# A transformer layer with relative attention and routed experts: other parts of the skewed tables, split terms stored once, shares spread by PE

## The chip, the core and the metric

The kernel runs on one core of a Trainium2 chip. The core has TensorE (PE, matrix products), VectorE (DVE), ScalarE (ACT), GpSimd (POOL), and SyncE (SP), which here issues nearly all DMAs; 16 DMA engines move the data between DRAM and on-chip memory (SBUF), and a DMA adds 16 to a semaphore when it has landed. The metric is the device time of one execution in microseconds; the figure of a kernel is the median of its runs.

## The reference

The input x is 4 batches x 1024 tokens x 256 channels. With LN a layer norm without scale:

```python
def attention(h):                        # h = LN(x)
    q, k, v = (heads(h @ W + b) for W, b in ((Wq, bq), (Wk, bk), (Wv, bv)))   # 16 heads of 16
    pos_k = heads(rel_embeddings @ Wk + bk)                                  # 128 buckets
    c2p[i, j] = (q @ pos_k.T)[i, bucket(i - j) + 64]     # clipped to 0..127, one bucket for all far keys
    p2c[i, j] = (k @ pos_k.T)[j, bucket(i - j) + 64]
    ctx = softmax((q @ k.T + c2p + p2c) / sqrt(48)) @ v
    out = ctx @ Wo + bo + h
    return LN(out) * ln_scale + ln_bias
def ffn(h):                              # every token goes to its best of 8 experts
    e = argmax(h @ Wr + br)
    return sum over i of relu((h if i == e else 0) @ W1[i] + b1[i]) @ W2[i] + b2[i]
x = x + LN(attention(LN(x)))
x = x + LN(ffn(LN(x)))
```

## The kernel before, in words

The program runs five stages, one after the other; each has a block of instructions for every engine, with the order of work written out by hand and semaphores between the engines.

**spread** makes the gathered position rows for all heads (pick_d). **project** takes 8 groups of 512 tokens: x is normalised (xn), turned, and multiplied by Wq, Wk and Wv. q and k are wanted to nearly full float32 precision in bfloat16 products, so each is split into three bfloat16 parts (hi, mid, lo). A product needs six terms, so that q is stored six times in split_d in the order hi hi hi mid mid lo, and k in the order that goes with it (QSLOTS and KSLOTS): 12 stores a group from L363. far_d (4 stores, L369) holds the products with the two buckets for far keys, v_d (L374) the values. POOL adds bo to xn, and SP stores that sum in xn_d (L352) for the residual later. On DVE, L435 and L403 make the rests for mid and lo, L400 and L406 those of the far rows. On SP every group's stores stand in one queue: xn_d of group s + 2, split_d and far_d of group s - 1, v_d of group s.

**attend** works on 64 units; a unit is one head of one batch. It is cut into 8 query tiles of 128. For each tile PE makes a table of 128 rows x 256 positions for each of q and k (L712, L714), and ACT copies it out of PSUM (L859). The table must be shifted by one column more in each row, which is done in DRAM: SP writes it to skew_d with one pitch (skew_write, L655) and reads it back with a pitch smaller by one (skew_read, L665, whose wait is at L662). A unit's table is written in two parts, tiles 0 to 3 and 4 to 7, and read in two parts, tiles 0 to 2 and 3 to 7 (PIECES), each for two tables. POOL then sets the edges of the bands (L926 to L942, five operations a part) and copies side values (L914). PE makes the scores (L733) and adds the bands by transposes (L740), DVE takes maxima (L814) and levels the bands (L833), PE transposes (L756, L763), ACT exponentiates (L865), PE multiplies with the values (L777). The row maxima of a unit are split in three bfloat16 parts by POOL (split_top, L952 to L962) and turned by PE (turn_top, L785), which stands in PE's order among the tables of a later unit.

SP's order for each unit u is: read part 1 of unit u + 1; write part 0 of unit u + 2; load the split and far rows of unit u + 4 (load_unit: two loads of 96 rows at L637, three of few rows at L642, into one of six buffers); store the result of unit u - 2 (L671); read part 0 of unit u + 2; write part 1 of unit u + 2. All of these pass through one queue, in which an instruction that waits holds all behind it.

**mix** takes 16 groups of two tiles: the sums of the probabilities are inverted, stored in share_d, and loaded back spread over the channels (share), beside heads, the stored xn and x. DVE multiplies heads by share (share_heads, L1156), PE multiplies by Wo (project_out, L1331), DVE adds the stored xn (residual, L1149), three norms and the routing follow. SP loads b1 (L1116) and, in its first eight steps, W2 (L1119). PE's constant_rows (L1361) gathers the constant part of the experts at steps 12 and 16. **experts** gathers the tokens by expert and computes the second layer.

## Time and profile before

| | |
|---|---|
| median of 3 runs | 2007.51 us (2007.21 to 2009.05) |
| profiled execution | 2003.63 us, span in the trace 2001.7 us, mean granted clock 0.916 |
| busy | PE 85%, PEld 58%, DVE 68%, ACT 56%, POOL 53% |
| DMA | 453.36 MB, mean 226 GB/s |
| stages | spread to 38, project to 200, attend to 1492, mix to 1688, experts to 2001 us |

The span is the trace's stretch from first to last work; the time of the execution is a little longer. Busy shares are means over stages that have different limits. In the page's own view of 40 slices the change between stages can be seen:

```profile
PE   1882389999999999999999999999973674999997
...
PEclk6996589999999999999999999999996675999998
```

One digit is one fortieth of the span, about 50 us, and 9 is 90% or more. Attention is the long row of nines in the middle, and mixing the dip after it.

### The profile page before, as it was taken

The page shows a single profiled execution, that of the slowest core. Times are in us where ns is not written, and L with a number is a line of the kernel's source. Part 1 is how long each engine was busy: PE and PEld are TensorE (multiplying, and loading weights), DVE is VectorE, ACT ScalarE, POOL GpSimd, SP SyncE. Part 2 cuts the span into 40 slices and gives each one's busy share as a digit, 9 for nine tenths or more (in the row PEclk, how much of TensorE's full clock was granted, in tenths as well). Part 3 has the DMA queues.
Part 4 walks back from the last instruction along what each step waited for, and adds up shares of the span by engine and source line. Part 5 has one row for each costly group of instructions (what it writes and reads, how often), then busy time and mean ns, then how long its engine had stood idle before and what let it go on. Part 6 is the DMA issues. An engine that isn't in the chain of part 4 may idle for free. (4 is left out here: it accounts for less than half of the span.)

```text
span 2001.7 us, 40568 instructions
## 1 busy us (share of the span) xinstructions
PE 1698.0 (85%) x13688; PEld 1159.6 (58%) x13688; DVE 1370.7 (68%) x3938; ACT 1121.8 (56%) x2233; POOL 1069.1 (53%) x1268
## 2 busy tenths in 40 slices
PE   1882389999999999999999999999973674999997
PEld 1451156565656566566565666566532464999996
DVE  1673188788888788898798899899843553343343
ACT  1672257676767677677677777677751460222221
POOL 0210267676777667667576777777711451233332
PEclk6996589999999999999999999999996675999998
DMA  4598778777777777777877777787718852676772
GB/s 113 188 303 274 225 250 262 246 237 251 245 261 248 256 247 240 257 254 245 265 237 251 249 261 250 240 272 246 235 44 215 284 176 86 198 212 215 223 219 78
DMA packets 320826, 453.36 MB, mean 226 GB/s; under 512 B 35132, under 2 KB 260303, under 8 KB 320526
## 3 DMA queue, kind: packets, MB, share of 16 engines
q1 hardware_dynamic: 308034, 415.25, 65.2%
q10 hardware_dynamic: 7596, 21.10, 3.4%
q0 software_dynamic: 4992, 14.43, 1.9%
q8 instruction: 112, 1.84, 0.4%
q14 instruction: 92, 0.75, 0.1%
HBM read 257.32 MB, written 193.65 MB: 225 GB/s over the span
## 5 line engine op out<-in xcount | busy, mean ns | idle before, releaser
L865 ACT ACTIVATE t_probsT<-t_flip 128x512 f32<-128x512 f32 x1024 | 619.2, 607 | 242.7 <-PE t_flip L756 117.5
L814 DVE TENSOR_REDUCE t_most<-t_scores 128x1 f32<-128x640 f32 (+1 forms) x512 | 436.7, 853 | 169.8 <-PE t_scores L740 166.5
L833 DVE TENSOR_SCALAR t_band<-t_band,t_top 128x384 f32<-128x384 f32 (+1 forms) x512 | 383.8, 750 | 0.0
L859 ACT COPY t_table<-t_table_ps 128x512 f32<-128x512 f32 x512 | 298.2, 582 | 70.7 <-issue 41.1
L777 PE MATMUL t_sum_ps<-t_probsT,t_vals 128*32 128x256 f32 x4096 | 329.5, 394 | 0.2 <-ACT t_probsT L865 0.2
L926 POOL TENSOR_TENSOR t_near<-t_near,t_masks 128x384 f32<-128x384 f32 (+1 forms) x128 | 146.8, 1147 | 338.9 <-DMA t_near<-skew_d 336.4
L942 POOL TENSOR_TENSOR t_near<-t_near,t_masks 128x768 f32<-128x768 f32 (+1 forms) x128 | 272.4, 2129 | 0.0
L763 PE MATMUL t_flip<-t_masks,t_band 128*128 128x128 f32 x1408 | 263.0, 276 | 0.0
L818 DVE CUSTOM_DVE_ANT_0 t_band<-t_scores,t_near 128x384 f32<-128x384 f32 (+1 forms) x512 | 262.1, 512 | 0.0
L740 PE MATMUL t_scores<-t_masks,t_near 128*128 128x128 f32 x1408 | 243.5, 277 | 7.1 <-POOLq L945 7.1
L733 PE MATMUL t_scores<-t_after,t_quest 105*128 105x256 bf16 (+3 forms) x1024 | 244.9, 289 | 2.6 <-DVE t_most L818 2.4
L740 PEld LDWEIGHTS t_scores<-t_masks,t_near 128*128 128x128 f32 x1408 | 182.7, 143 | 46.6 <-POOLq L945 8.7
L712 PE MATMUL t_table_ps<-t_rows,t_quest 96*128 96x256 bf16 x512 | 143.5, 280 | 69.1 <-DMA t_before<-far_d 49.8
L733 PE MATMUL t_scores<-t_before,t_quest 105*128 105x256 bf16 (+3 forms) x768 | 195.0, 294 | 0.0
L763 PEld LDWEIGHTS t_flip<-t_masks,t_band 128*128 128x128 f32 x1408 | 164.7, 143 | 4.8
L756 PE MATMUL t_flip<-t_quest,t_before 108*128 108x512 bf16 (+3 forms) x512 | 161.4, 316 | 0.8 <-ACT t_probsT L865 0.7
L756 PE MATMUL t_flip<-t_quest,t_after 108*128 108x512 bf16 (+3 forms) x512 | 158.7, 310 | 1.2 <-DMA t_quest<-t_topT 0.8
L1606 PE MATMUL e_hid_ps<-e_xT,e_w 128*128 128x128 f32 x1248 | 148.0, 278 | 5.6 <-DMA e_total<-total_d 5.2
L1606 PEld LDWEIGHTS e_hid_ps<-e_xT,e_w 128*128 128x128 f32 x1248 | 147.5, 194 | 8.2 <-issue 5.5
L939 POOL TENSOR_TENSOR t_near<-t_near,t_masks 128x384 f32<-128x384 f32 (+1 forms) x128 | 145.5, 1137 | 0.0
L714 PE MATMUL t_table_ps<-t_rows,t_after 96*128 96x256 bf16 x512 | 142.9, 279 | 0.0
L1588 PE MATMUL e_out_ps<-w_all,e_hid 128*128 x624 | 141.0, 379 | 0.0
(186 smaller groups left out, 2343.7 us busy)
## 6 DMA issues: line engine op xcount, KB each, us to landing
skew_d<-t_table SPq DMA_DIRECT2D x128, 1024.0 KB, 8.9
t_near<-skew_d SPq DMA_DIRECT2D x128, 640.0 KB, 6.2
t_near<-skew_d SPq DMA_DIRECT2D x128, 384.0 KB, 4.8
e_w<-in_L_ffn_W_dram ACTq DMA_DIRECT2D x39, 512.0 KB
e_w<-in_L_ffn_W_dram SPq DMA_DIRECT2D x39, 512.0 KB
split_d<-p_part SPq DMA_DIRECT2D x32, 384.0 KB
t_after<-split_d SPq DMA_DIRECT2D x64, 192.0 KB
t_quest<-split_d SPq DMA_DIRECT2D x64, 192.0 KB
```

The lines of the kernel that those rows point to most:

```text
L733: nc.tensor.matmul(out[:, at:at + size], quest[i][0:XROWS, t * P:(t + 1) * P], keys[0:XROWS, piece[0] * P:piece[0] * P + size], start=at % ...
L740: last = nc.tensor.matmul(out[:, (j - lo) * P:(j - lo + 1) * P], near[n % 2][:, 1, j, (t - j + 1) * P:(t - j + 2) * P], ident, start=False ...
L756: last = nc.tensor.matmul(out[:, (a - lo) * P:(z - lo) * P], keys[:, j * P:(j + 1) * P], quest[i][:, a * P:z * P], start=first, stop=False ...
L763: last = nc.tensor.matmul(out[:, (t - lo) * P:(t - lo + 1) * P], band[n % 2][:, t, at:at + P], ident, start=False, stop=True, is_transpose ...
L777: last = nc.tensor.matmul(sum_ps[32 * g:32 * g + 32, 0:2 * P], vals[b % 2][:, j, h * VDIM:h * VDIM + 32], probsT[s % 3][:, g * 2 * P:(g + ...
L814: nc.vector.tensor_reduce(most[:, c, 1:2], out[:, wide:S], AX.X, ALU.max)
L818: nc.vector.tensor_tensor_reduce(band[n % 2][:, t, 0:wide], out[:, 0:wide], near[n % 2][:, 0, t, at:at + wide], 1.0, -3.0e38, ALU.add, ALU ...
L833: nc.vector.tensor_scalar(band[n % 2][:, t, 0:wide], band[n % 2][:, t, 0:wide], top[n % 2][:, t:t + 1], None, ALU.subtract).then_inc(level ...
L859: nc.scalar.copy(table[n % 2][:, h, :, u % 4, :], table_ps[:, :, :]).then_inc(table_kept, 1)
L865: nc.scalar.activation(probsT[s % 3][:, half * 512:(half + 1) * 512], flip_ps[half][:, :], ACT.Exp, scale=SCALE).then_inc(expd, 1)
L942: nc.gpsimd.tensor_tensor(tail, tail, masks[:, 1, :].unsqueeze(1).unsqueeze(1).to_broadcast([P, 2, many, P]), ALU.mult).then_inc(edge_made, 1)
L1606: last = nc.tensor.matmul(hid_ps[s % 2][:, c, :], w1[s % WB][:, f, c * P:(c + 1) * P], xT[s % 2][:, f, :], start=(f == 0), stop=(f == 1))
```

## The change

In **attend** the table of a unit is written in parts of five and three tiles (TILES), and read in parts of four and four (PIECES). POOL's steps for the edges move later, and the split of the maxima, which stood between two parts of the edges, now comes before the second one's first step. The split rows are loaded by six DMAs of 32 rows each instead of two of 96. In **project** each of the three parts is stored once: q's as mid, lo, hi and k's as hi, mid, lo, so that a load finds any pair of neighbours; the pair of one part twice is a step of 0 in the load. far_d gets one store with padding. The sum xn + bo is no longer made or stored, and POOL has nothing to do there. In **mix** the shares are loaded once, as 16 rows, and PE spreads them over the channels by a product with a 0/1 matrix (which), for each group; PE also adds bo, by a product of one row; the residual is made from x and the kept inverse deviations (inv_all, which project now writes for all tokens). W2's loads stand at every second step, and the second constant_rows at step 18. The padding, masks and experts are as they were.

```diff
-QSLOTS = ((0, 1, 3), (3, 1, 2), (5, 1, 1))
-KSLOTS = ((1, 2, 3), (2, 2, 2), (0, 1, 1))
+QSLOTS = ((0, 1, 5), (2, 3), (4,))
+KSLOTS = ((0, 2, 4), (1, 3), (5,))
...
-        split_d = dram("split_d", [2, TERMS, N * DH, S], BF16)
-        far_d = dram("far_d", [2, N, 2, PARTS, S], BF16)
+        split_d = dram("split_d", [2, PARTS, N * DH, S], BF16)
+        far_d = dram("far_d", [B, 4, 32, PARTS, S], BF16)
...                                                       project, SP
-                    sp.wait_ge(xnb_made, g + 1)
-                    sp.dma_start(view(xn_d, g * G * D, [[D, P], [P * D, GT], [1, D]]), xnb[g % 2][:, :, :]
-                                 ).then_inc(xn_out[g % 2], 16)
...
-                        for n, (first, step, many) in enumerate((QSLOTS, KSLOTS)[m // 2]):
-                            at = ((m // 2 * TERMS + first) * (N * DH) + b * D + m % 2 * P) * S + half * G
-                            sp.dma_start(view(split_d, at, [[S, P], [step * N * DH * S, many], [1, G]]),
-                                         part[g % 2][:, n, m, :].unsqueeze(1).to_broadcast([P, many, G])
-                                         ).then_inc(split_out[g % 2], 16)
+                        mine = at + m // 2 * (PARTS * part_at) + m % 2 * (P * S)
+                        takes = ((0, 2, 1), (2, 3, 0)) if m < 2 else ((0, 3, 0),)
+                        for a, z, slot in takes:
+                            sp.dma_start(view(split_d, mine + slot * part_at, [[S, P], [part_at, z - a], [1, G]]),
+                                         part[g % 2][:, a:z, m, :]).then_inc(split_out[g % 2], 16)
...
-                    for m in range(4):
-                        at = (m // 2 * N + b * H + m % 2 * 8) * 2 * PARTS * S + half * G
-                        sp.dma_start(view(far_d, at, [[PARTS * S, 16], [S, PARTS], [1, G]]),
-                                     far_part[g % 2][32 * m:32 * m + 16, :, :]).then_inc(far_out[g % 2], 16)
+                    sp.dma_start(view(far_d, b * (P * PARTS * S) + half * G, [[PARTS * S, P], [S, PARTS], [1, G]]),
+                                 far_part[g % 2][:, :, :]).then_inc(far_out[g % 2], 16)
...                                                       project, POOL
-                nc.gpsimd.tensor_tensor(xnb[g % 2][:, :, :], xn[g % NB][:, :, :],
-                                        bo_b[:, :].unsqueeze(1).to_broadcast([P, GT, D]), ALU.add).then_inc(xnb_made, 1)
...                                                       attend
-    PIECES = ((0, 3), (3, QT))
-    EDGES = ((0, 3), (3, QT - 1))
+    TILES = ((0, 5), (5, QT))
+    PIECES = ((0, 4), (4, QT))
+    EDGES = ((0, 4), (4, QT - 1))
...
+            pair, one, both = [[S, 2 * DH], [1, S]], [[S, DH], [1, S]], [[part, 2], [S, DH], [1, S]]
...
-                for dst, side_at in ((after[i], TERMS * part), (quest[i], 0)):
-                    sp.dma_start(dst[0:KROWS, :], view(split_d, side_at + n * (DH * S), [[part, TERMS], [S, DH], [1, S]])
-                                 ).then_inc(hats_in[i], 16)
...
+                for dst, src_at, dims in ((after[i][0:2 * DH, :], at_k, both), (after[i][2 * DH:4 * DH, :], at_k, both),
+                                          (after[i][4 * DH:KROWS, :], at_k, [[2 * part, 2]] + one),
+                                          (quest[i][0:2 * DH, :], at_q + part, [[0, 2]] + one),
+                                          (quest[i][2 * DH:4 * DH, :], at_q + 2 * part, [[0, 2]] + one),
+                                          (quest[i][4 * DH:KROWS, :], at_q, both)):
+                    sp.dma_start(dst, view(split_d, src_at, dims)).then_inc(hats_in[i], 16)
...
-                sp.wait_ge(table_kept, n * QT + 4 * h + 4)
+                lo, hi = TILES[h]
+                sp.wait_ge(table_kept, n * QT + hi)
...
-                    sp.wait_ge(scored, (n - 2) * QT + 4 * h + 4)
-                    sp.wait_ge(seen, (n - 2) * QT + 4 * h + 4)
+                    sp.wait_ge(scored, (n - 2) * QT + TILES[h][1])
+                    sp.wait_ge(seen, (n - 2) * QT + TILES[h][1])
...
-            steps = ((2, 0, (0, 1)), (3, 0, (2,)), (4, 0, (3,)), (5, 0, (4,)),
-                     (6, 1, (0, 1)), (7, 1, (2,)), (8, 1, (3,)), (9, 1, (4,)))
+            steps = ((3, 0, (0, 1)), (4, 0, (2,)), (5, 0, (3,)), (6, 0, (4,)), (8, 1, (0, 1)), (9, 1, (2, 3)), (10, 1, (4,)))
...                                                       mix
-                for k in range(2):
-                    n = g // 4 * H + k * 8
-                    sp.dma_start(share[i][:, k, :], view(share_d, n * S + g % 4 * (2 * P), [[S, 8], [0, DH], [1, 2 * P]])
-                                 ).then_inc(heads_in[i], 16)
...
-                sp.dma_start(xn[i][:, :, :], rows_of(xn_d, g)).then_inc(xn_in[i], 16)
...
+            sp.dma_start(share[:, :, :], view(share_d, 0, [[S, H], [H * S, B], [1, S]])).then_inc(share_in, 16)
...
-                nc.vector.tensor_tensor(y1[g % BUFS][:, :, :], out_ps[g % 2][:, :, :], xn[g % BUFS][:, :, :],
-                                        ALU.add).then_inc(y1_made, 1)
+                for t in range(G):
+                    tile = g * G + t
+                    last = nc.vector.scalar_tensor_tensor(y1[g % BUFS][:, t, :], xt[g % XBUFS][:, t, :],
+                                                          inv_all[:, tile:tile + 1], out_ps[g % 2][:, t, :], ALU.mult, ALU.add)
...
+                    last = nc.tensor.matmul(out_ps[g % 2][:, t, :], masks[0:1, 3, :], bo_row[:, :], start=False, stop=True)
...
+                for k in range(2):
+                    last = nc.tensor.matmul(share_ps[g % 2][:, k, :], which[:, k, :], share[:, b, at:at + G * P],
+                                            start=True, stop=True)
```

On SP in the even part of attention, one unit of before (skew_d is the table in DRAM, t_near the shifted band, t_after and t_quest the rows of keys and queries):

```order
L665 DMA t_near<-skew_d 128x5x256 x2
L655 DMA skew_d<-t_table 256x1x1024
L637 DMA t_after<-split_d 96x1x1024
L637 DMA t_quest<-split_d 96x1x1024
L642 DMA t_quest<-far_d 6x1024
L642 DMA t_after<-far_d 3x1024
L642 DMA t_before<-far_d 3x1024
L671 DMA ctx_d<-t_made 128x256
L665 DMA t_near<-skew_d 128x3x256 x2
L655 DMA skew_d<-t_table 256x1x1024
```

And the same place after the change:

```order
L658 DMA t_near<-skew_d 128x4x256 x2
L648 DMA skew_d<-t_table 256x1x1280
L628 DMA t_after<-split_d 32x1x1024 x3
L628 DMA t_quest<-split_d 32x1x1024 x3
L634 DMA t_quest<-far_d 6x1024
L634 DMA t_after<-far_d 3x1024
L634 DMA t_before<-far_d 3x1024
L664 DMA ctx_d<-t_made 128x256
L658 DMA t_near<-skew_d 128x4x256 x2
L648 DMA skew_d<-t_table 256x1x768
```

The order of kinds is the same; two loads became six, and the parts of the reads and writes have other sizes.

On POOL in attention, from the first part's third edge step on, before:

```order
L934 TENSOR_TENSOR t_near<-t_near,t_side 128x4x128
L952 CAST t_top_part<-t_top 128x8
L954 TENSOR_TENSOR t_top_rest<-t_top,t_top_part 128x8
L957 CAST t_top_part<-t_top_rest 128x8
L959 TENSOR_TENSOR t_top_rest<-t_top_rest,t_top_part 128x8
L962 CAST t_top_part<-t_top_rest 128x8
L914 COPY t_side<-t_table 128x2x4
L939 TENSOR_TENSOR t_near<-t_near,t_masks 128x4x128
L942 TENSOR_TENSOR t_near<-t_near,t_masks 128x2x4x128
```

And after:

```order
L936 TENSOR_TENSOR t_near<-t_near,t_masks 128x2x4x128
L946 CAST t_top_part<-t_top 128x8
L948 TENSOR_TENSOR t_top_rest<-t_top,t_top_part 128x8
L951 CAST t_top_part<-t_top_rest 128x8
L953 TENSOR_TENSOR t_top_rest<-t_top_rest,t_top_part 128x8
L956 CAST t_top_part<-t_top_rest 128x8
L908 COPY t_side<-t_table 128x2x3
L920 TENSOR_TENSOR t_near<-t_near,t_masks 128x3x128
L923 TENSOR_TENSOR t_near<-t_near,t_side 128x3x128
L928 TENSOR_TENSOR t_near<-t_near,t_side 128x3x128
```

The split of the maxima (t_top_part, t_top_rest) stood inside the second part's edge steps (sizes of four tiles), behind its L926, and stands now between the first part's last step and the second part's first one (L920, three tiles).

On SP in the projection stage, one group of before:

```order
L363 DMA split_d<-p_part 128x3x512
L363 DMA split_d<-p_part 128x2x512
L363 DMA split_d<-p_part 128x512
L363 DMA split_d<-p_part 128x3x512
L363 DMA split_d<-p_part 128x2x512
L363 DMA split_d<-p_part 128x512
...
L369 DMA far_d<-p_far_part 48x1x512 x4
L374 DMA v_d<-p_v_1 128x4x288
```

And of after:

```order
L361 DMA split_d<-p_part 128x2x512
L361 DMA split_d<-p_part 128x512
L361 DMA split_d<-p_part 128x2x512
L361 DMA split_d<-p_part 128x512
L361 DMA split_d<-p_part 128x3x512 x2
L364 DMA far_d<-p_far_part 384x1x512
L369 DMA v_d<-p_v_1 128x4x288
```

A group had 12 stores of split_d and 4 of far_d and has now 6 and 1; the store of xn_d between the groups is gone.

## Rows read from the trace of the kernel before

**Rows 1.** Stretch: busy PE, PEld, DVE, ACT, POOL; clock; DMA share; GB/s. Then L763.

```profile
300.00:1440.00 1140.00, 1087.80 (x9996) 684.91 (x9992) 990.45 (x2839) 829.45 (x1595) 813.06 (x1008) 0.99 0.77 250
L763 PE MATMUL t_flip<-t_masks,t_band 128*128 128x128 f32 x1301 | 243.4, 276 | 0.0
```

**Rows 2.** Waits of SP's queue, 300 to 1440 us: sum, count, longest.

```profile
SPq L662 <- DMA skew_d<-t_table: 695.8, 115, 8.3
```

**Rows 3.** Timeline of SP, 795 to 830 us: start, duration.

```profile
797.43 0.93 SPq L665 DMA_DIRECT2D t_near<-skew_d  x2
798.46 0.56 SPq L655 DMA_DIRECT2D skew_d<-t_table  x1
799.07 0.77 SPq L637 DMA_DIRECT2D t_after<-split_d  x1
...
808.00 0.91 SPq L665 DMA_DIRECT2D t_near<-skew_d  x2
809.02 0.57 SPq L655 DMA_DIRECT2D skew_d<-t_table  x1
816.39 0.93 SPq L665 DMA_DIRECT2D t_near<-skew_d  x2
```

**Rows 4.** Waits of PE and POOL, 300 to 1440 us.

```profile
PE t_table_ps L785 <- POOL t_top_part L962: 45.1, 44, 4.4
POOL t_near L926 <- DMA t_near<-skew_d: 307.5, 106, 6.1
```

**Rows 5.** Busy time in short stretches, columns as in rows 1.

```profile
808.00:808.25 0.25, 0.00 (x0) 0.00 (x0) 0.25 (x2) 0.00 (x0) 0.17 (x2) 1.00 0.38 147
...
808.50:808.75 0.25, 0.00 (x0) 0.00 (x0) 0.24 (x1) 0.00 (x0) 0.17 (x2) 1.00 0.39 139
...
810.00:811.00 1.00, 1.00 (x7) 0.85 (x6) 0.00 (x0) 0.47 (x1) 1.00 (x2) 0.50 0.82 213
813.00:814.00 1.00, 1.00 (x13) 0.42 (x6) 0.96 (x6) 0.13 (x1) 0.26 (x1) 0.80 1.02 415
```

**Rows 6.** Timeline of PE at 215 us.

```profile
214.98 0.37 PE L712 MATMUL t_table_ps<-t_rows,t_quest 96*128 96x256 bf16 x1 [49.79 <-DMA t_before<-far_d]
```

**Rows 7.** Timeline of SP, 155 to 200 us.

```profile
156.85 9.76 SPq L363 DMA_DIRECT2D split_d<-p_part  x12
...
169.30 0.58 SPq L374 DMA_DIRECT2D v_d<-p_v  x1
...
192.82 2.60 SPq L369 DMA_DIRECT2D far_d<-p_far_part  x4
199.86 0.35 SPq L676 DMA_DIRECT2D t_rows<-pick_d  x1
```

**Rows 8.** Timelines of PE and DVE in the projection stage.

```profile
69.76 3.70 PE L524 MATMUL p_qk_ps<-p_xT,p_wq 128*128 128x512 f32 x8
...
82.15 1.13 PE L524 MATMUL p_qk_ps<-p_xT,p_wq 128*128 128x512 f32 x2
70.12 2.28 DVE L435 TENSOR_TENSOR p_rest<-p_qk,p_part 128x2048 f32<-128x2048 f32 x1
...
79.93 2.86 DVE L406 TENSOR_TENSOR p_far_part<-p_far_rest,p_far_part 128x512 bf16<-128x512 f32 x1
...
85.77 2.28 DVE L435 TENSOR_TENSOR p_rest<-p_qk,p_part 128x2048 f32<-128x2048 f32 x1
170.79 2.29 DVE L435 TENSOR_TENSOR p_rest<-p_qk,p_part 128x2048 f32<-128x2048 f32 x1 [4.36 <-ACT p_part L501]
...
177.25 0.69 DVE L406 TENSOR_TENSOR p_far_part<-p_far_rest,p_far_part 128x512 bf16<-128x512 f32 x1
```

**Rows 9.** Mixing stage: a wait, busy time, PE by line (x, busy, mean ns).

```profile
DVE m_headsT L1156 <- DMA m_share<-share_d: 51.2, 14, 12.8
1500.00:1690.00 190.00, 109.63 (x520) 86.89 (x520) 90.26 (x330) 65.75 (x148) 60.86 (x50) 0.63 0.61 180
L1331 PE MATMUL m_out_ps<-m_wo,m_headsT 128*128 128x256 f32 x128 | 49.8, 556 | 63.3 <-DVE m_headsT L1156 63.3
```

More of the change, by code:

```diff
@@ L83, in constants @@
     steps[:, ET + 8 + P:] = np.arange(NT)[None, :] * P + np.arange(P)[:, None] + 1
+    heads = np.zeros((H, 2, P), np.float32)
+    for h in range(H):
+        heads[h, h // 8, h % 8 * DH:h % 8 * DH + DH] = 1.0
     sel = np.zeros((P, E), np.float32)
@@ L208, in _ @@
             for tab in range(2):
-                for n, (first, step, many) in enumerate((KSLOTS, QSLOTS)[tab]):
-                    for slot in range(first, first + step * many, step):
+                for n, slots in enumerate((KSLOTS, QSLOTS)[tab]):
+                    for slot in slots:
                         for c in range(2):
@@ L265, in _, with project @@
             nc.vector.tensor_tensor(part[:, 2, :, :, :], rest[:, :, :, :], part[:, 1, :, :, :], ALU.subtract).then_inc(dve_made, 1)
-def project(nc, sem, spent, x, Wq, bq, Wk, bk, Wv, bv, bo, c_masks, posT_d, xn_d, split_d, far_d, v_d):
+def project(nc, sem, spent, x, Wq, bq, Wk, bk, Wv, bv, c_masks, posT_d, split_d, far_d, v_d, inv_all):
     G = 512
@@ L347, in _ @@
                 load(g)
[L348 to L355 removed]
+            for s in range(NG + 1):
+                if live(s + XB):
+                    load(s + XB)
                 g = s - 1
@@ L559, in attend @@
     BUFS = 6
-    HATS = 5
+    HATS = 9
     FAR = KROWS + PARTS
@@ L586, in attend @@
         vals = [sb(f"vals{i}", [P, QT, VROW]) for i in range(2)]
-        table = [sb(f"table{i}", [P, 2, 2, 4, SPOT]) for i in range(2)]
+        table = [sb(f"table{i}", [P, 2, QT, SPOT]) for i in range(2)]
         side = [sb(f"side{i}", [P, 2, QT]) for i in range(2)]
@@ L1016, in mix @@
         out_ps = [ps(f"out_ps{i}", [P, G, D]) for i in range(2)]
+        share_ps = [ps(f"share_ps{i}", [P, 2, G * P]) for i in range(2)]
         xf_ps = ps("xf_ps", [P, 2, G * P])
@@ L1107, in _ @@
                      (wr[:, :, :], Wr.rearrange("(k p) n -> p k n", p=P)),
-                     (br_b[:, :], row(br, E)), (steps[:, :], c_steps)]
-            assert len(loads) == 7
+                     (br_b[:, :], row(br, E)), (steps[:, :], c_steps),
+                     (which[:, :, :], c_heads), (bo_row[:, :], view(bo.tensor, 0, [[D, 1], [1, D]]))]
+            assert len(loads) == 9
             for dst, src in loads:
                 sp.dma_start(dst, src, allow_slow_non_contiguous=True).then_inc(loaded, 16)
-            for g in range(BUFS):
-                load(g)
+            load(0)
+            load(1)
+            sp.wait_ge(inverse_made, 1)
+            sp.dma_start(share_d[:, :].rearrange("n (a v) -> (n a) v", a=2), inverse[:, :]).then_inc(share_out, 16)
+            load(2)
+            sp.wait_ge(share_out, 16)
+            sp.dma_start(share[:, :, :], view(share_d, 0, [[S, H], [H * S, B], [1, S]])).then_inc(share_in, 16)
+            load(3)
             for dst, src in [(b1_sb[:, :, :], b1.rearrange("e (c p) -> p e c", p=P)), (b2_sb[:, :], b2),
```

155 lines of the change are left out of this document (76 added, 79 removed).

## The prediction

> **What bounds the kernel now.** I read the granted-clock and busy table by stretch first. From 300 to 1440 us, where the attention stage runs evenly, PE is busy 1087.8 of 1140.0 us at clock 0.99 and the DMA engines 0.77 [rows 1]. That looks like a PE-bound stage, so I read the waits of the SP queue for the same stretch: its reads back of the skewed tables (L662) waited 695.8 us for the writes (skew_d<-t_table) to land, 115 times [rows 2]. The SP timeline shows why this decides [rows 3]: read 797.43, write 798.46, unit loads from 799.07, read 808.00, write 809.02, the next read 816.39. Every write follows its read in about 0.1 us and every read waits for the write ahead of it. This is a closed ring of DMAs with nothing of PE in it: 816.39 - 797.43 = 18.96 us for one unit (a unit is one head of one batch, 64 in all). The stretch holds 1301 / 22 = 59.1 units by the transposes of L763, 22 to a unit [rows 1], so a unit takes 19.3 us and PE's own work is 1087.8 / 59.1 = 18.4 us of it. PE follows the ring: its one large stall is 45.1 us at L785, for the split of the row maxima on POOL, which itself sits behind POOL's wait for t_near from DMA, 307.5 us [rows 4].
>
> The next view is the same table in quarters of a microsecond just after a large write has landed. At 808.00 only unit loads are left to run, for the read issued at 808.00 shows from 809 on; there the share of the 16 DMA engines is 0.38, at 147 GB/s, then 0.39 at 139 at 808.5 [rows 5]. 6 / 16 = 0.375. At 813 us, with table traffic, the share is 1.02 at 415 GB/s. The load's source pattern is `[[part, 6], [S, 16], [1, S]]`: its outermost size is 6, and six engines carry it, at 147 / 6 = 24.5 GB/s each.
>
> **The change, part by part.**
> Unit loads, the largest term. The two loads of 96 rows become six of 32 rows, each with an outermost size of 2 in the source (the middle of the change). The bytes stay: 2 x 96 x 2048 = 393,216. If the outermost size sets the engines, as 6 gave six, each of these runs on two; and I take the same two for all six, since the two loads of before share one set of six (two sets would show 0.75). Then it is 393,216 / (2 x 24.5 GB/s) = 8.0 us, in place of 393,216 / 147 GB/s = 2.7 us. In the ring they stand between the large write and the next read, and on the engines that carry them the read's packets stand behind them, so the difference, 5.3 us, comes onto the ring. Its cover is nothing: the ring has no slack [rows 3]. From below: the two slow engines do their part of the read while the other fourteen are idle, and could do it faster; the 64 rows of it per engine take 4 us at the mean rate, so at most 1 us comes back, 4.3. From above: 393,216 bytes at 2 x 23 GB/s (139 / 6, the lowest share of such a window that I take) is 8.5 - 2.7 = 5.8. I take 5.3, because the other side of the packet queue is equally loaded before and after. 62 of the 64 rounds of the ring have a load: 62 x 5.3 = +329 us (267 to 360). The first unit's load delays the first table too, for which PE waits until 214.98 [rows 6]: +5.
>
> The Trainium skill has this as a rule (DMA: Bandwidth & Descriptors, "Why a DMA increments its semaphore by 16 and not by 1"): a DMA runs on the largest number of engines up to 16 that divides the outermost size of both patterns. For 6 and 96 that is six, which the share of 0.38 bears out; for 2 and 32 it is two, always the lowest-numbered, which no run here has shown yet. By it the term is the same.
>
> The parts of five and three tiles move bytes and no sum: before, a read of 5 + write of 4, then a read of 3 + write of 4; now 4 + 5 and 4 + 3. Nine tiles and seven tiles either way: 0. Four more issues a unit on SP, at 0.77 us each [rows 3], run inside the 9.5 us wait for the large write: 0, at most +1 us a round if they outlast it.
>
> Maxima ahead of masking: POOL's split no longer stands behind the part that waits longest for t_near. The 45.1 us of stall at L785 [rows 4] go, and what is late next is the same DMA at the scores (L740): the ring sets the round, so 0 in the even stretch. Once, at the end, PE is some tiles further ahead: -4 us (0 to -8). The first write needs a fifth tile: +1.
>
> Projection stage. SP issues without a gap from 156.85 to the end: 12 stores of split_d 9.76 us, 4 of far_d 2.60, one of v_d 0.58, 13 us a group, the last at 192.82 + 2.60, and attention begins at 199.86 [rows 7]. The last lo part is ready at 177.25, when L406 follows it on DVE [rows 8], so SP is 18 us late. Now a group has 6 stores at 9.76 / 12 = 0.81 each, one of far_d and one of v_d, about 6 us: SP is no longer the limit. PE is: a group of it runs from 69.76 to 82.15, 12.4 us. DVE has the same room, since its L406 took 2.86 us beside the POOL addition, which goes, and 0.69 us without it [rows 8]. L435 of group 0 starts at 70.12 and that of group 1 at 85.77, or at 83.6 without the 2.2 us of L406; then 6 x 12.4 to that of group 7 at 158.0, and 6.5 us from there to the end of lo (170.79 to 177.25 in the trace) give 164.5; six stores 4.9, far_d 0.65 and the same 4.4 us to the first DMA of attention: 174.5 against 199.86, -25 us. Bounds: -30 (SP's whole excess and the backlog) and -18 (a group at 13.4 us, as 85.77 less 70.12 without L406's 2.2).
>
> Mixing stage. The loads of m_share and m_xn go. DVE waited 51.2 us for m_share, of which 12.8 behind the load of single b1 words, which stays, and about 10 for the first shares, which a spread by PE behind the same store and load doesn't shorten; 28 us is the most to win. Against it stand 128 more PE passes of 256 columns (the share's and bo's): at the 556 ns of L1331 71 us, on a PE that is busy 109.6 of 190 us at clock 0.63 [rows 9]. At the half clock PE would be the limit, at +5; nearer its full one the steps take 6 to 6.5 us where they took 7.2 over eleven groups. I take -15 (-28 to +5), the middle. W2's loads at every second step and the constant rows at step 18 lie beside this: 0.
>
> **The sum.** The profiled execution took 2003.63 us with 2001.7 of span; 2003.6 - 25 + 5 + 1 + 329 - 4 - 15 = 2294.6. The median of the runs before is 2007.51, 3.9 above it: 2298, say 2300.
>
> **Rivals.**
> Two engines (chance 0.82): the above. Its own range, from the bounds of its terms taken two thirds of the way, is 2235 to 2340.
> The engines don't follow the outermost size, and the loads stay at six or more (0.09). For it: only one size, six, is seen [rows 5]. Against: 0.375 fits no other count. Then 2003.6 - 25 + 2 - 4 - 15 = 1962, +3.9 = 1966, faster. It decides from the point where six small loads take less than 3 us together. Were they to run on all 16, the ring would fall under PE's 18.4 us and PE would set it: 62 x 0.9 less, about 1910.
> The loads run on two engines but on different pairs, or largely beside the tables (0.05): 1 to 3 us a round, 2 x 62 = 124: 2090. For it: queues can interleave; against it: the loads come after the write, not with it [rows 5].
> The clock (0.04): the large stall ended at 809, and at 810 to 811 us PE was granted 0.50, its lower level of 1.2 GHz [rows 5]. With a stall of 6 us in each round the clock could stay at its half. PE's 18.4 us would become 36.8 with the clock always low, over the ring's 24.5; with it low half of the time 27.6, so 2300 + 62 x 3.1 = 2490.
>
> **How the numbers follow.** Two engines, pairs and clock are slower: 0.91, less 0.01 that a half-right mixture lands within 0.2%, which is about what a measurement of this kernel can tell from no change (4 us). Faster 0.09. The range holds 8 in 10: 2210 to 2370 holds nearly all of the first case's 0.82 and leaves out the rest.
>
> **What the profile after would show.** Right: the wait from the small write to its read up from 7.4 to about 12.7 us and from the large write to its read still about 9.5, a round of 24 us, PE busy about 0.75 of the even stretch with its idle time at L740 behind POOL, none at L785; just after the large write a share of 0.12 to 0.13 at 46 to 49 GB/s for several microseconds; attention's first DMA at 175 us; DVE's L406 at 0.7 us; no wait for m_share, and steps of 6 us in mixing. Wrong: a round of 19 us or less, or a share of 0.38 in that window. If the stores of split_d still hold ACT, the 25 us fail alone; if PE's half clock holds in mixing, the 15 do.

## The result and the profile after

| | before | after |
|---|---|---|
| median on the same chip | 2007.36 us | 2223.32 us |
| ratio | | 1.108 (95% interval 1.106 to 1.111) |
| span of the profiled execution | 2001.7 us | 2222.9 us |

The kernel became slower by 11%, where 15% were forecast. By SP's first DMA of each stage the two spans divide as follows; the forecast is the sum of the prediction's terms for that stage.

| stage | before | after | difference | forecast |
|---|---|---|---|---|
| spread and project | 199.9 | 172.3 | -27.6 | -25 |
| attend | 1292.9 | 1498.1 | +205.2 | +331 |
| mix | 196.3 | 239.5 | +43.2 | -15 |
| experts | 312.6 | 313.0 | +0.4 | 0 |

Attention was forecast 126 us too high and mixing 58 us too low. So the total stands inside the range because two errors had opposite signs: with mixing as forecast it would have been 2165, below the range of 2210 to 2370. That part is luck. The rows of after, in the order of the rows of before. The even part of attention first (columns as in [rows 1]):

```profile
300.00:1600.00 1300.00, 1120.12 (x9750) 688.58 (x9749) 969.59 (x2768) 812.98 (x1558) 789.37 (x985) 0.94 0.68 215
```

PE is busy 1120 of 1300 us, 0.86, where it was 0.95, and the DMA engines' share fell from 0.77 to 0.68. The waits of SP's queue there:

```profile
SPq L655 <- DMA skew_d<-t_table: 511.9, 97, 8.8
SPq L648 <- ACT t_table L852: 62.0, 81, 2.4
```

The read still waits above all for the table to land; its waits are 5.3 us each, fewer and shorter than the 6.0 of [rows 2], because SP itself now issues for longer. SP's timeline of one unit (start, duration):

```profile
1008.20 0.91 SPq L658 DMA_DIRECT2D t_near<-skew_d  x2
1009.21 0.55 SPq L648 DMA_DIRECT2D skew_d<-t_table  x1
1009.82 1.94 SPq L628 DMA_DIRECT2D t_after<-split_d  x3
1011.80 3.71 SPq L628 DMA_DIRECT2D t_quest<-split_d  x3
...
1017.35 0.35 SPq L664 DMA_DIRECT2D ctx_d<-t_made  x1
1019.27 1.15 SPq L658 DMA_DIRECT2D t_near<-skew_d  x2
1020.52 1.86 SPq L648 DMA_DIRECT2D skew_d<-t_table  x1
1030.77 0.91 SPq L658 DMA_DIRECT2D t_near<-skew_d  x2
```

The wait from the large write (1009.21, five tiles) to its read (1019.27) is 10.1 us, that from the small write (1020.52) to its read (1030.77) 10.3; [rows 3] had 9.5 and 7.4. Over 300 to 1400 us the means are 9.0 and 10.3, where before had 9.7 and 7.4: the cost of the slow loads appears behind the small write, where it was forecast, as 10.3 and not 12.7. A unit takes 22.6 us. The six loads take 5.65 us to issue where two took 1.6. The ring also has PE in it now: SP waits 62.0 us in 1300, about 1 us a round, for ACT's copy of the table (L648 above), and before that wait was 4 us in 1100. The shares in this unit, columns as in [rows 5]:

```profile
1008.00:1009.00 1.00, 1.00 (x10) 0.75 (x7) 0.97 (x4) 0.80 (x2) 1.00 (x2) 1.00 0.00 0
1019.00:1020.00 1.00, 1.00 (x11) 0.83 (x9) 1.00 (x1) 0.71 (x2) 1.00 (x1) 1.00 0.14 51
1027.00:1028.00 1.00, 1.00 (x15) 0.64 (x8) 1.00 (x2) 0.74 (x3) 0.00 (x0) 1.00 0.14 48
1028.00:1029.00 1.00, 1.00 (x9) 0.65 (x7) 0.65 (x5) 1.00 (x3) 0.25 (x1) 1.00 0.14 55
1029.00:1030.00 1.00, 1.00 (x14) 0.55 (x14) 0.87 (x2) 0.50 (x1) 1.00 (x2) 1.00 0.12 46
1030.00:1030.50 0.50, 0.50 (x6) 0.35 (x4) 0.47 (x3) 0.30 (x1) 0.50 (x2) 1.00 0.02 6
```

From 1027 to 1030 the share is 0.12 to 0.14 at 46 to 55 GB/s: two of 16 engines carry all that is left, and the read follows when they end. The forecast had this share just after the large write; it is there at 1019 and lasts for several microseconds only behind the small one. The 0.14 at 1019 us is a second thing to see: two engines work on while the large write's landing is answered and the next read starts up, a pause in which nothing else runs. At 1008 us the same pause has a share of 0.00. PE and POOL wait as follows:

```profile
POOL t_near L920 <- DMA t_near<-skew_d: 482.3, 63, 11.8
PE t_scores L733 <- POOLq L939: 172.6, 58, 5.8
```

L785 (now L778) is gone from PE's list, as forecast, and the scores wait for POOL's edges, behind DMA, in its place. The projection stage, SP and one row of DVE:

```profile
154.58 2.98 SPq L361 DMA_DIRECT2D split_d<-p_part  x6
157.60 0.86 SPq L364 DMA_DIRECT2D far_d<-p_far_part  x1
158.51 1.07 SPq L369 DMA_DIRECT2D v_d<-p_v  x1
162.77 2.97 SPq L361 DMA_DIRECT2D split_d<-p_part  x6
...
172.29 0.34 SPq L669 DMA_DIRECT2D t_rows<-pick_d  x1
```

```profile
80.13 0.69 DVE L400 TENSOR_TENSOR p_far_part<-p_far_rest,p_far_part 128x512 bf16<-128x512 f32 x1
```

A group's stores take 2.98 + 0.86 + 1.07 = 4.9 us on SP, against 12.9 in [rows 7], and attention begins at 172.29. The additions on far rows are at 0.69 us at once. The mixing stage, two stretches and PE's lines:

```profile
1750.00:1770.00 20.00, 20.00 (x50) 13.04 (x50) 8.61 (x34) 8.10 (x20) 9.14 (x8) 0.50 0.53 162
1790.00:1810.00 20.00, 20.00 (x56) 13.95 (x56) 8.61 (x34) 7.42 (x17) 6.49 (x6) 0.50 0.51 158
```

```profile
L1326 PE MATMUL m_out_ps<-m_wo,m_headsT 128*128 128x256 f32 x128 | 63.8, 651 | 4.2 <-DVE m_headsT L1151 4.2
L1328 PE MATMUL m_out_ps<-m_bo_row,m_masks 1*128 1x256 f32 x64 | 37.9, 692 | 0.0
L1336 PE MATMUL m_share_ps<-m_share,m_which 16*128 16x256 f32 x64 | 29.6, 615 | 24.3 <-DMA m_share<-share_d 24.3
```

PE is busy for the whole of each stretch at clock 0.50, its lower level, where before had 0.63 over the stage and PE busy for 58% [rows 9]. The product with Wo (L1326) went from 556 to 651 ns, and a step takes 8.9 us early in the stage and 10.5 later, where 6 were forecast.

### The profile page after: what moved, and what is told of

Its sections match the earlier page's. It is cut to its first block and busy times, and to the rows that moved or that the text cites. A ratio compares the mean times of both kernels' runs of the same rounds, so it can differ in the third digit from the quotient of the medians.

```text
span 2222.9 us, 40953 instructions
## 1 busy us (share of the span) xinstructions
PE 1840.6 (83%) x13816; PEld 1223.9 (55%) x13816; DVE 1362.5 (61%) x3954; ACT 1124.4 (51%) x2233; POOL 1041.9 (47%) x1260
## 5 line engine op out<-in xcount | busy, mean ns | idle before, releaser
L733 PE MATMUL t_scores<-t_masks,t_near 128*128 128x128 f32 x1408 | 259.0, 290 | 195.0 <-POOLq L939 195.0
L920 POOL TENSOR_TENSOR t_near<-t_near,t_masks 128x512 f32<-128x512 f32 (+1 forms) x128 | 146.3, 1143 | 530.3 <-DMA t_near<-skew_d 530.1
L826 DVE TENSOR_SCALAR t_band<-t_band,t_top 128x384 f32<-128x384 f32 (+1 forms) x512 | 374.2, 731 | 0.0
L770 PE MATMUL t_sum_ps<-t_probsT,t_vals 128*32 128x256 f32 x4096 | 344.1, 409 | 0.2 <-ACT t_probsT L858 0.2
L756 PE MATMUL t_flip<-t_masks,t_band 128*128 128x128 f32 x1408 | 273.5, 284 | 0.0
L936 POOL TENSOR_TENSOR t_near<-t_near,t_masks 128x1024 f32<-128x1024 f32 (+1 forms) x128 | 268.9, 2100 | 0.0
L726 PE MATMUL t_scores<-t_before,t_quest 105*128 105x256 bf16 (+3 forms) x768 | 204.3, 308 | 0.0
L756 PEld LDWEIGHTS t_flip<-t_masks,t_band 128*128 128x128 f32 x1408 | 170.9, 147 | 6.2
L749 PE MATMUL t_flip<-t_quest,t_before 108*128 108x512 bf16 (+3 forms) x512 | 166.3, 326 | 0.8 <-ACT t_probsT L858 0.7
L749 PE MATMUL t_flip<-t_quest,t_after 108*128 108x512 bf16 (+3 forms) x512 | 163.2, 319 | 1.6 <-DMA t_quest<-t_topT 1.2
L933 POOL TENSOR_TENSOR t_near<-t_near,t_masks 128x512 f32<-128x512 f32 (+1 forms) x128 | 145.6, 1138 | 0.0
```

What stands on the lines that cost most here:

```text
L726: nc.tensor.matmul(out[:, at:at + size], quest[i][0:XROWS, t * P:(t + 1) * P], keys[0:XROWS, piece[0] * P:piece[0] * P + size], start=at % ...
L733: last = nc.tensor.matmul(out[:, (j - lo) * P:(j - lo + 1) * P], near[n % 2][:, 1, j, (t - j + 1) * P:(t - j + 2) * P], ident, start=False ...
L749: last = nc.tensor.matmul(out[:, (a - lo) * P:(z - lo) * P], keys[:, j * P:(j + 1) * P], quest[i][:, a * P:z * P], start=first, stop=False ...
L756: last = nc.tensor.matmul(out[:, (t - lo) * P:(t - lo + 1) * P], band[n % 2][:, t, at:at + P], ident, start=False, stop=True, is_transpose ...
L770: last = nc.tensor.matmul(sum_ps[32 * g:32 * g + 32, 0:2 * P], vals[b % 2][:, j, h * VDIM:h * VDIM + 32], probsT[s % 3][:, g * 2 * P:(g + ...
L826: nc.vector.tensor_scalar(band[n % 2][:, t, 0:wide], band[n % 2][:, t, 0:wide], top[n % 2][:, t:t + 1], None, ALU.subtract).then_inc(level ...
```

## Experiments

Names: a16 is the changed kernel and b the kernel before, each with other unit loads; the numbers behind b say what the outermost size is. Attend and mix are the stages' durations in the profiled execution, in us; the ratio is to the kernel before, timed on the same chip.

| kernel | median | ratio (95%) | attend | mix |
|---|---|---|---|---|
| b2 | 2240.4 | 1.121 (1.118 to 1.123) | 1529.1 | 197.8 |
| b3 | 2110.7 | 1.056 (1.054 to 1.059) | 1401.5 | 194.8 |
| b16 | 1999.0 | 0.997 (0.996 to 0.999) | 1287.6 | 197.6 |
| b16_six | 1995.4 | 0.995 (0.993 to 0.997) | 1285.3 | 195.3 |
| a16 | 2017.8 | 1.010 (1.007 to 1.013) | 1295.2 | 236.0 |
| a16_nobo | 1954.1 | 0.976 (0.972 to 0.981) | 1294.6 | 178.0 |
| a16_bo128 | 1949.8 | 0.973 (0.970 to 0.976) | 1285.4 | 173.8 |
| a16_all128 | 1963.5 | 0.979 (0.976 to 0.982) | 1297.5 | 182.5 |
| a16_parts4 | 1960.2 | 0.977 (0.974 to 0.980) | 1242.5 | 232.9 |
| a16_oldorder | 2014.0 | 1.005 (1.003 to 1.007) | 1296.7 | 239.7 |
| p4_bo128_new | 1967.6 | 0.981 (0.978 to 0.984) | 1311.0 | 171.2 |
| p4_bo128 | 1896.3 | 0.945 (0.942 to 0.947) | 1238.5 | 172.2 |

Four kernels have the same attend code (a16, a16_nobo, a16_bo128, a16_all128): 1285 to 1298 us. So differences of attend under some 12 us are not read. Four have the same mixing code (after, a16, a16_parts4, a16_oldorder): 233 to 240 us.

SP's timeline from 300 to 1400 us gives the ring of each kernel, as means in us: from the start of the large write (the one with the loads behind it; with parts of four tiles both writes have one size) to its read, from the small write to its read, from a read to the next write (twice a round), and the whole round.

| kernel | large write to read | small write to read | read to write | round |
|---|---|---|---|---|
| before | 9.7 | 7.4 | 1.1 | 19.3 |
| b16 | 9.6 | 7.3 | 1.2 | 19.2 |
| b16_six | 9.6 | 7.2 | 1.2 | 19.2 |
| b3 | 9.7 | 9.1 | 1.1 | 21.0 |
| b2 | 9.5 | 10.8 | 1.3 | 23.0 |
| after | 9.0 | 10.3 | 1.6 | 22.6 |
| a16 | 9.1 | 8.0 | 1.1 | 19.3 |
| a16_oldorder | 9.1 | 8.0 | 1.1 | 19.3 |
| a16_parts4 | 9.1 | 7.1 | 1.2 | 18.5 |
| p4_bo128 | 9.1 | 7.1 | 1.2 | 18.4 |
| p4_bo128_new | 8.9 | 6.7 | 1.95 | 19.5 |

### Do two engines make the loss?

a16 changes the order of rows in each load, and the rows of pick_d with it:

```diff
-            pair, one, both = [[S, 2 * DH], [1, S]], [[S, DH], [1, S]], [[part, 2], [S, DH], [1, S]]
+            two = lambda step: [[S, DH], [step, 2], [1, S]]
...
-                for dst, src_at, dims in ((after[i][0:2 * DH, :], at_k, both), ...
+                for dst, src_at, dims in ((after[i][0:2 * DH, :], at_k, two(part)), ...
```

> The changed kernel, with the order of rows inside each load of 32 turned round (channel first, then part), so that the outermost size of the source is 16 and not 2; bytes and number of loads stay. Two-engine theory (a round is the work of the busiest DMA engine plus a gap): the busiest engine has 12.6 + 1.0 us in place of 12.6 + 8.2, the ring falls below PE's 18.4 us, PE sets a round of about 18.6, attention takes 1255 us in place of 1498, total about 1980 (1965 to 1995). Rival, that six issues a unit on SP or the parts of five and three tiles cost the time: attention stays near 1498, total 2220.

The total is 2017.8, and attend 1295.2 against 1498.1 in after: 203 us for nothing but the order of rows inside the loads. The rival that six issues or the parts make the loss is out for these 203 us. But attention stayed 40 us above the 1255 that was expected, so something else in the change costs time too.

b2 and b3 do it from the other side:

```diff
-                    sp.dma_start(dst[0:KROWS, :], view(split_d, side_at + n * (DH * S), [[part, TERMS], [S, DH], [1, S]])
-                                 ).then_inc(hats_in[i], 16)
+                    for a in range(0, TERMS, 2):                       # b3: 3, and [part, 3]
+                        sp.dma_start(dst[a * DH:(a + 2) * DH, :],
+                                     view(split_d, side_at + n * (DH * S) + a * part, [[part, 2], [S, DH], [1, S]])
+                                     ).then_inc(hats_in[i], 16)
```

> The kernel before, with each load of 96 rows cut into three loads of 32 rows with an outermost size of 2; nothing else changed. Two-engine theory: attention 205 us longer as in the changed kernel, total 2212 (2195 to 2230). Rival, that the other edits of attention cost the time: 2007 to 2015.

> The kernel before, with each load of 96 rows cut into two loads of 48 rows with an outermost size of 3. If a round is the busiest engine's work plus one gap (12.6 + 393,216 / (3 x 24.5 GB/s) = 5.35, + 1.8 = 19.8 us, against 19.1 to 19.3 before): +0.6 a round, total 2045 (2030 to 2060). If the loads add their full length to the ring, as the prediction had it: 5.35 - 2.7 = 2.65 a round, total 2171. If engines don't matter: 2007.

b2 added 236 us to attend, more than the 205 expected, and the share just before a read shows two engines again:

```profile
934.00:935.00 1.00, 1.00 (x9) 0.69 (x7) 0.78 (x5) 1.00 (x3) 0.51 (x1) 1.00 0.14 55
935.00:936.00 1.00, 1.00 (x14) 0.50 (x13) 0.80 (x2) 0.82 (x3) 1.00 (x2) 1.00 0.13 53
```

b3 lies at +109 us, between both numbers that were expected (+38 and +164). Its share at such a place is 3 / 16, at 74 GB/s, three times 24.5:

```profile
931.00:931.50 0.50, 0.50 (x9) 0.47 (x6) 0.50 (x2) 0.50 (x1) 0.50 (x2) 1.00 0.18 74
```

The mean rounds of SP's ring are 19.3 us in before (size 6), 21.0 in b3 and 23.0 in b2. The loads' own time by their bytes, an estimate at 24.5 GB/s an engine, is 2.7, 5.35 and 8.0 us. So 2.65 us more of load cost 1.7, and 5.3 more cost 3.7. Nearly all of it stands behind the small write (7.4, 9.1 and 10.8 us); the wait behind the large write, where the loads are, did not grow (9.7, 9.7, 9.5).

b16 takes the size up instead, with the same two DMAs:

```diff
-view(split_d, side_at + n * (DH * S), [[part, TERMS], [S, DH], [1, S]])
+view(split_d, side_at + n * (DH * S), [[S, DH], [part, TERMS], [1, S]])
```

> The kernel before, with its two loads of 96 rows in another order of rows (channel first, then term): the outermost size is 16 and not 6, the same two DMAs and bytes. If the ring of DMAs bounds an even round of before (19.2 us) and the loads stand on it, it falls to PE's 18.4 to 18.6: attention 40 to 55 us less, total 1950 to 1965. If six engines' 2.7 us are hidden in the pause between a landed write and the read behind it, and PE's own work and stalls bound the round: attention within 10 us of before, total 1995 to 2005.

The second expectation held: 5 us, which is under what can be read. Sixteen engines would need 1.0 us for the loads (an estimate, 393,216 bytes at 16 x 24.5 GB/s) and gained next to nothing over six engines' 2.7 us, so those 2.7 us were covered all along. The cover can be seen. A read is issued at 916.25, and half a microsecond later the engines are all but idle, where before had 0.39 half a microsecond after its read of 808.00 [rows 5]:

```profile
916.75:917.00 0.25, 0.23 (x2) 0.16 (x2) 0.00 (x0) 0.00 (x0) 0.25 (x2) 1.00 0.06 20
```

The loads are gone from the pause, and the kernel gained nothing by it, although the ring was still closed (SP waited 676.9 us in 1100 for writes to land, in 113 waits). The even stretch looks as it did in before:

```profile
300.00:1400.00 1100.00, 1049.91 (x9687) 660.78 (x9680) 942.81 (x2750) 804.05 (x1547) 790.99 (x979) 0.99 0.78 252
```

### What else does the change cost or gain in attention?

a16_parts4 takes a16 and puts TILES back to (0, 4), (4, 8), PIECES to three and five tiles with EDGES to match, and POOL's steps to the list of before.

> The kernel of a16, with the parts of the table and POOL's order of before (written in four and four tiles, read in three and five, the split of the maxima behind the second part's first edge step). By the prediction the parts and the order are worth 4 us at the end and nothing in the even stretch: attention 1295 to 1303 in place of 1295, total 2018 to 2026. Rival, that the new parts cost time (their second wait is 8.5 to 10 us where before had 7.4) and the order gains nothing: attention 1255 to 1275. Rival, that the order's gain is real and hidden by the cost of loads: attention 1320 or more.

Attend is 1242.5 us, shorter than in any of the three cases expected and 53 us shorter than a16. The parts and the order are not worth 4 us, they cost 53. PE is now busy for 98% of the even stretch, and its wait for the split of the maxima is small although the order is that of before:

```profile
300.00:1400.00 1100.00, 1077.46 (x10055) 680.27 (x10052) 997.77 (x2850) 829.62 (x1596) 811.62 (x1000) 1.00 0.77 255
```

```profile
PE t_table_ps L778 <- POOL t_top_part L956: 13.9, 17, 3.0
```

a16_oldorder separates sizes from order:

```diff
-            steps = ((3, 0, (0, 1)), (4, 0, (2,)), (5, 0, (3,)), (6, 0, (4,)), (8, 1, (0, 1)), (9, 1, (2, 3)), (10, 1, (4,)))
+            steps = ((2, 0, (0, 1)), (3, 0, (2,)), (4, 0, (3,)), (5, 0, (4,)),
+                     (6, 1, (0, 1)), (7, 1, (2,)), (8, 1, (3,)), (9, 1, (4,)))
```

> The kernel of a16 (parts of five and three tiles, read in four and four), with POOL's order of before: edges of part 0 one tile earlier, the split of the maxima behind the second part's first step. a16 has attention of 1295 us, and 1242.5 with parts and order of before. If the order costs the 50 us: 1240 to 1255, total 1960. If the sizes of the parts do (four tiles of edges in part 0, 7.2 us of POOL ahead of the first scores, and a write of five tiles ahead of the read): 1285 to 1310, total 2010 to 2030.

With the new sizes the order makes no difference to the time (1296.7 and 1295.2); it only decides where PE waits. In a16_oldorder PE waits for the split, in a16 for the edges at the scores:

```profile
PE t_table_ps L778 <- POOL t_top_part L956: 41.3, 38, 2.5
```

```profile
PE t_scores L733 <- POOLq L939: 47.7, 38, 4.6
```

The ring shows where the sizes cost: the wait behind the large write is 9.1 us in all three kernels, that behind the small one 8.0 us with the new sizes and 7.1 with the old. A write of three tiles behind a read of four lands 0.9 us later than a write of four behind a read of three, though both pairs move seven tiles; 62 x 0.9 is 56 us, by estimate.

p4_bo128_new has the new order with the old sizes (and bo as below, which doesn't touch attention).

> The kernel of p4_bo128 with POOL's new order alone (the split of the maxima ahead of the second part), parts as before. PE waits 13.9 us in 1100 for the split in a16_parts4: at most 15 us to win. If the order gains what the prediction gave it: -4 (0 to -8), total 1893. If the later edges (one tile later in part 0, two in part 1) make PE wait at the scores: attention 10 to 50 us longer than in p4_bo128, total 1910 to 1950.

Here the new order costs 72 us (1311.0 against 1238.5), more than expected. POOL now stands at the split until the unit's last maximum is there, with the second part's edges behind it; in p4_bo128 it waited 19.1 us there and 234.2 for the reads at L921. The writes land sooner than in p4_bo128 (8.9 and 6.7 us), but SP waits for ACT's copies before it can issue them, so here the DMAs alone no longer set the round:

```profile
POOL t_top_part L947 <- DVE t_peak L819: 303.6, 56, 5.4
PE t_scores L734 <- POOLq L940: 63.9, 56, 1.3
SPq L649 <- ACT t_table L853: 92.2, 84, 2.8
```

So the sizes cost 54 us with the old order, the order 72 with the old sizes, and both together only 53. The two are not independent, and neither gains anything alone. The order itself is two edits, the split ahead of the second part and the edge steps one or two tiles later; no run takes them apart.

b16_six asks why a16_parts4 is 45 us faster in attend than b16, where parts and order are the same:

> The kernel of b16 (before, outermost size 16), with six loads of 32 rows in place of two of 96: the form of the loads in a16_parts4, from the six stored terms. a16_parts4 has the parts and POOL's order of before and yet attention of 1242.5 us against 1287.6 in b16. If the form of the loads makes this (they are issued more slowly behind the large write): attention 1240 to 1255, total 1950 to 1965. If that each part is stored and read from one place makes it: attention stays at 1280 to 1295, total 1990 to 2005.

The form of the loads is not the cause: 1285.3. PE waits as long for the split as in before:

```profile
PE t_table_ps L787 <- POOL t_top_part L964: 40.0, 44, 3.2
```

What is left between b16_six (1285.3) and a16_parts4 (1242.5) is that each part is stored once and read from one place, the table's other layout in SBUF (all tiles behind one another for each of q and k), far_d's padding, and what project's shorter stage leaves behind. Which of these gives the 43 us was not tried and stays open. The rows say where it shows: the wait behind the large write is 9.1 us and not 9.6, the round 18.5 and not 19.2, and a read of five tiles, of the same 640 KB, lands in 5.6 us (median) and not in 6.4.

### What made mixing slower?

a16_nobo leaves bo out of the result:

```diff
-                                         wo[:, k, :], start=(k == 0), stop=False)
-                    last = nc.tensor.matmul(out_ps[g % 2][:, t, :], masks[0:1, 3, :], bo_row[:, :], start=False, stop=True)
+                                         wo[:, k, :], start=(k == 0), stop=(k == 1))
```

> The kernel of a16 without PE's products of one row for bo (bo is left out of the result): 64 passes of 0.6 us less in the mixing stage. If PE at its half clock bounds that stage, the stage is 35 to 40 us shorter than in a16, total 38 us under a16. If the one-row products also keep the clock low, the clock rises without them and it is 60 us or more. If the steps are bound elsewhere (DVE, ACT, DMA): under 5 us.

The stage is 58 us shorter, just under the 60 of the expectation with the clock and more than the 36.9 us for which these products kept PE busy in a16, and PE's clock rises. One stretch of a16 and two of a16_nobo:

```profile
1566.00:1586.00 20.00, 20.00 (x55) 13.92 (x55) 9.19 (x42) 7.78 (x18) 6.49 (x6) 0.50 0.53 159
```

```profile
1505.00:1525.00 20.00, 16.17 (x51) 10.64 (x49) 17.41 (x63) 11.91 (x28) 14.28 (x13) 0.78 0.55 170
1525.00:1545.00 20.00, 19.45 (x90) 15.18 (x90) 15.64 (x64) 12.98 (x31) 12.81 (x11) 0.80 0.80 246
```

a16_bo128 keeps the products and makes them tall:

```diff
+    heads[:, 2] = 1.0 / P                                    # heads is now 128 x 3 x 128
-                    last = nc.tensor.matmul(out_ps[g % 2][:, t, :], masks[0:1, 3, :], bo_row[:, :], start=False, stop=True)
+                    last = nc.tensor.matmul(out_ps[g % 2][:, t, :], which[:, 2, :], bo_row[:, :], start=False, stop=True)
```

> The kernel of a16, with the product for bo made over 128 rows (128 rows of ones/128 by 128 copies of bo) and not over one row: the same number of products and of columns, no work less. If it is the number of passes that bounds PE in mixing, the stage stays at 236 us, total 2018. If products of one row keep PE's clock at its half level, the clock rises as without bo, to 0.74 to 0.84 in the early steps, and the stage takes 185 to 200 us, total 1970 to 1980.

This is the cleanest of the runs: as many products, of as many columns, on 128 rows and not on one, and the stage went from 236.0 to 173.8 us, shorter than expected.

```profile
1500.00:1520.00 20.00, 17.19 (x75) 12.41 (x74) 17.77 (x66) 12.46 (x29) 14.18 (x12) 1.00 0.52 160
1520.00:1540.00 20.00, 18.88 (x106) 15.49 (x105) 16.92 (x71) 14.94 (x33) 13.56 (x12) 1.00 0.89 279
```

```profile
L1327 PE MATMUL m_out_ps<-m_wo,m_headsT 128*128 128x256 f32 x128 | 36.8, 412 | 6.1 <-DVE m_headsT L1152 6.1
L1329 PE MATMUL m_out_ps<-m_bo_row,m_which 128*128 128x256 f32 x64 | 20.1, 397 | 0.0
L1337 PE MATMUL m_share_ps<-m_share,m_which 16*128 16x256 f32 x64 | 19.5, 431 | 25.3 <-DMA m_share<-share_d 25.3
```

The clock is 1.00 in these stretches, where a16 had 0.50, and bo's product takes 397 ns where after had 692. The other two kernels with this mixing code have 171.2 and 172.2 us.

a16_all128 does the same for the shares.

> The kernel of a16_bo128, with the product that spreads the shares made over 128 rows too (the 16 rows of shares loaded eight times, the 0/1 matrix divided by 8) and not over 16. If the clock is a matter of rows used, it rises further than in a16_bo128: the mixing stage another 5 to 15 us shorter. If only the one-row products mattered: the same as a16_bo128, at most 3 us longer by the seven more loads.

Inconclusive: the stage is 8.7 us longer than in a16_bo128. The eight loads of shares in place of one made the first product wait for 40 us, not 25:

```profile
1506.97 3.68 PE L1339 MATMUL m_share_ps<-m_share,m_which 128*128 128x256 f32 x8 [40.27 <-DMA m_share<-share_d]
```

From that product to the end of the stage it took 144.8 us (1651.8 - 1507.0), in a16_bo128 151.1 (1630.4 - 1479.3). The height of the shares' product may be worth 6 us; the loads cost 15.

### The best version

> What the runs so far recommend together: loads with outermost size 16, parts and POOL's order of before, bo over 128 rows. Stages add up: project 170 to 171, attention 1242, mixing 174, experts 312.6: span 1899, total 1895 to 1905. Rival: the gain of one stage is lost in the next, total above 1920.

1896.3 us, 5.5% faster than before (0.945, 0.942 to 0.947) and some 15% under after's 2223; the stages did add up.

```profile
300.00:1400.00 1100.00, 1082.08 (x10099) 683.39 (x10098) 997.68 (x2856) 833.53 (x1604) 812.89 (x1001) 1.00 0.78 256
```

PE is busy for 98% of the even stretch at full clock, so at most 2% is left to win there without less work for PE. The ring is no looser: SP's reads still waited for a write to land 107 times in this stretch. The two limits now lie together.

## Why the prediction was right, and where it wasn't

**Two engines.** Right as a mechanism: the loads' outermost size of 2 makes 203 us of the loss by itself (after against a16), and the shares read 2 / 16, 3 / 16 and 6 / 16 for sizes 2, 3 and 6. The rule of the Trainium skill (DMA: Bandwidth & Descriptors, "Why a DMA increments its semaphore by 16 and not by 1") agrees with all three. That it is the lowest-numbered engines no row tells, but that all six loads share the same two is shown by 0.14 where other pairs would have given more.

**The size of that term.** The step that failed is "Its cover is nothing: the ring has no slack". +329 us (267 to 360) measured as 203 to 236, under the term's own lower bound. SP has no slack, but the engines have: between the landing of a write and the first packets of the next read there is a pause, 0.00 at 1008 us and two engines busy at 1019. b16 shows that six engines' 2.7 us were wholly under such cover. Of longer loads a part still was: 2.65 us more cost 1.7 in b3, and 5.3 more cost 3.7 in b2. The wait behind the small write grew and the other did not, as forecast, but to 10.3 us and not to 12.7. The row that was used for it (0.38 at 808.00) showed this cover: SP had already issued the read, and the loads ran where the read's packets had not begun.

**Parts and order.** The second step that failed, and the larger error of thought: "move bytes and no sum" was right for the bytes and wrong for the time. The parts cost 54 us, and the ring has them in one place: the write behind the read of four tiles lands 0.9 us a round later (8.0 against 7.1). Why seven tiles take longer when four of them are read and three written wasn't tried. PE's waits follow: 41.3 us in 1100 at the split or 47.7 at the scores, where a16_parts4 has 13.9. For the order I counted the stall that goes and not what the split itself waits for: the last maximum. With the old sizes POOL waits 303.6 us for it, where in p4_bo128 it waited about 260 in all, and the time is 72 us longer; the later edge steps are part of that, in a share that no run shows. How the two together come to only 53 I can't derive from the rows.

**What was not in the sum at all**: some 43 us of gain in attention from the stored parts or the table's layout (a16_parts4 against b16_six). From before to after by way of b16, b16_six, a16_parts4 and a16 the steps are -5, -2, -43, +53 and +203. They add up to the +205 by construction, each being the difference of two neighbours, so this sum tests nothing; it says which terms were missed, and that -43 and +53 hid each other. The -5 and -2 are under what can be read.

**Projection.** -27.6 against -25, and by the steps given: DVE's L406 at 0.69 us, SP no longer late, attention's first DMA at 172.3 against 174.5 forecast.

**Mixing.** +43.2 against -15. The step that failed is "I take -15 (-28 to +5), the middle". Its upper bound, "at the half clock PE would be the limit, at +5", is given without working, and the only price beside it is the 556 ns of L1331, a mean over both levels (clock 0.63). At clock 0.50 the products take 0.62 to 0.69 us, PE's busy time went from 109.6 to 190.6 us, and its 100% of steps of 8.9 to 10.5 us set the stage. And I took the clock as given, where the change itself held it down: with bo's products on 128 rows the stage is 22.5 us shorter than before, inside the range of that term.

**Rivals.** That the engines don't follow the outermost size is out. The clock did cost time in mixing. In attention it was 0.94 in the even stretch, where before had 0.99, and PE's work of a unit was 19.4 us and not 18.4 (1120.12 us over 57.6 rounds), still under the ring's 22.6, so there it is at most a small part. "Largely beside the tables", 1 to 3 us a round, is partly what happened: 3.3 us a round in the changed kernel (203 / 62) and 3.8 in b2 (236 / 62), of the 5.3 forecast.

## What to carry to other kernels

Look at the outermost size of both sides of each DMA: an order of rows that costs nothing to choose decided between 2, 3 and 6 engines here, or more, and was worth 203 us. Move the loads' rows so that the outermost size is large, and the rows of the other factor of the product with them. When loads seem to lie on a ring, ask what else runs in the pause after a landing, and test by making them faster, not only slower. When a stall is to be removed by a new order, list what the moved instruction itself waits for. And a product of one row is not free: made over 128 rows with the same count of passes it saved 62 us.

## What the runs showed of the hardware that was not expected

- In after PE's clock stood at 0.50 from 1690 to 1830 us while PE was busy for 17.5 to 20 of every 20 us, the last 80 us without a gap, with one pass in nine on one row (64 of the 576 of L1326, L1328, L1336, L1346, L1355 and L1366; 37.9 us of its time); with the same passes on 128 rows it stood at 1.00 from 1500 to 1540 us.
- The issue of a DMA on SP has no fixed price: six loads of 32 rows took 5.65 us in after (1.94 + 3.71), 0.94 each, where two of 96 rows took 0.8 each in before, and a write of skew_d took 1.86 us at 1020.52 and 0.55 at 1009.21, in the same unit. What sets it was not tried.
- A load of outermost size 16 was no faster for the kernel than one on 6 engines (5 us of 1293), while 3 engines cost 109 us and 2 engines 236. That size 16 ran on all sixteen no row shows by itself; its loads were over sooner (0.06 where size 6 had 0.39).
- From the issue of a write of 3 tiles behind a read of 4 to the read that waits for it took 8.0 us (a16), with 4 written behind 3 read 7.1 (a16_parts4), though each pair moves the same bytes.
